# Weight splits as they land, output sums ahead of expert choice, token scales ahead of ranks, and the last routing in the count step's head

## The reference, cut to what matters

```python
x = L0_attn_x                                  # (4, 2048, 256)
xn = layernorm(x)
# gated linear attention, 8 heads, DK = 128, DV = 64
q = xn @ Wq ; k = (xn @ Wk) * DK**-0.5 ; v = xn @ Wv
alpha = sigmoid((xn @ Wg + bg) / 16)           # one per token and head
state = alpha_t * state + k_t (x) v_t          # over the 2048 tokens, in order
out_t = q_t . state
att = (out * sigmoid(xn @ Wog)) @ Wo
# mixture of experts: E = 64, 8 groups, the best 4 groups, the best 8 experts, CAP = 256
scores = sigmoid(xn @ gate_w.T) ; sfc = scores + gate_bias
# groups by the sum of their two best, then the best 8 experts among the 4 best groups
w = 2.5 * scores[chosen] / sum(scores[chosen])
# every expert takes its first 256 tokens of the 8192, in token order
ffn = sum over chosen experts of w * (silu(t @ w_gate) * (t @ w_up)) @ w_down
return x + att + ffn
```

## Time and profile before

| What | us |
|---|---|
| three runs, median (lowest to highest) | 1458.67 (1458.36 to 1460.96) |
| the profiled execution | 1454.37 |
| its span, first to last instruction | 1452.7 |
| mean granted TensorE clock, share of full | 0.976 |
| PE busy in the span | 1320.8 |
| DVE busy | 960.7 |
| ACT busy | 552.4 |

### The profile page before, as it was taken

One profiled execution on the slowest core, in us unless ns is written; L12 is line 12 of the kernel. 1 busy time (PEld: TensorE's weight loads), 2 busy tenths in 40 slices (PEclk: granted clock), 3 DMA queues, 4 the chain that ended last, 5 costly groups with the idle time before them and its releaser, 6 DMA issues.

```text
span 1452.7 us, 27616 instructions
## 1 busy us (share of the span) xinstructions
PE 1320.8 (91%) x9460; PEld 1143.8 (79%) x9460; DVE 960.7 (66%) x2425; ACT 552.4 (38%) x1079; POOL 530.6 (37%) x407
## 2 busy tenths in 40 slices
PE   2999888998989899989999999999999999999992
PEld 2778777786878687778888888888888888888872
DVE  4766777867775666857757577575775757757450
ACT  4555555545554342223333333333333333333220
POOL 3001001000100006735636456364563645636422
PEclk9989999999999999999999999999999999999996
DMA  5338433434332131125646566465564655646666
GB/s 201 128 124 266 137 122 125 163 106 135 124 136 96 66 94 59 59 84 152 150 138 154 130 152 148 135 154 133 148 147 136 156 135 154 151 140 151 178 216 219
DMA packets 134513, 203.48 MB, mean 140 GB/s; under 512 B 12400, under 2 KB 106160, under 8 KB 134320
## 3 DMA queue, kind: packets, MB, share of 16 engines
q1 hardware_dynamic: 108208, 161.10, 34.3%
q0 software_dynamic: 26240, 41.63, 14.9%
HBM read 153.33 MB, written 57.74 MB: 145 GB/s over the span
## 4 chain that ended last, share of the span: by engine, by line
PE 66%; DVE 15%; issue 6%; DMA 5%; ACT 4%; SPq 1%; POOL 1%; DVEq 1%; POOLq 0%; ACTq 0%
PE bank L672 16%; PE bank L791 6%; PE bank L747 6%; PE bank L767 6%; PE bank L684 5%; PE bank L714 4%; PE bank L732 4%; PE bank L800 4%; PE bank L696 3%; PE bank L735 3%; PE bank L705 3%; DMA out_dram<-arena 3%; DVE Dt L1251 2%; PE bank L617 2%; PE bank L781 2%
## 5 line engine op out<-in xcount | busy, mean ns | idle before, releaser
L540 POOL DMA_INDIRECT arena<-table,idx_all x132 | 167.7, 1270 | 271.6 <-DVE arena L1354 208.7
L548 POOL DMA_INDIRECT acc<-arena,idx_all x128 | 224.9, 1757 | 78.3 <-DMA acc<-arena,idx_all 42.2
L672 PE MATMUL bank<-xp,wq 128*128 128x512 f32 x768 | 210.2, 409 | 0.0
L672 PE MATMUL bank<-xp,wk 128*128 128x512 f32 x768 | 208.1, 407 | 0.0
L672 PEld LDWEIGHTS bank<-xp,wk 128*128 128x128 f32 x768 | 142.4, 192 | 32.0 <-issue 0.2
L1251 DVE TENSOR_TENSOR_SCAN Dt<-decay,eye_b 128x512 f32<-128x512 f32 x128 | 156.7, 1226 | 2.3 <-DMA decay<-decay_dram 2.3
L672 PEld LDWEIGHTS bank<-xp,wq 128*128 128x128 f32 x768 | 137.6, 191 | 25.5
L714 PE MATMUL bank<-qT,kT 128*128 128x128 f32 x1024 | 136.8, 277 | 2.7 <-ACT kT L954 2.7
L747 PEld LDWEIGHTS bank<-V,kw 128*128 128x128 f32 x960 | 121.0, 193 | 15.1 <-issue 10.6
L714 PEld LDWEIGHTS bank<-qT,kT 128*128 128x128 f32 x1024 | 125.2, 193 | 5.0 <-ACT kT L954 4.5
L747 PE MATMUL bank<-V,kw 128*128 128x64 f32 x960 | 128.2, 277 | 0.0
(11 more groups left out here) (152 smaller groups left out, 2200.0 us busy)
## 6 DMA issues: line engine op xcount, KB each, us to landing
decay<-decay_dram SPq DMA_DIRECT2D x64, 512.0 KB, 5.5
carry<-decay_dram SPq DMA_DIRECT2D x60, 512.0 KB, 4.6
arena<-in_L_attn_x_dram SPq DMA_DIRECT2D x16, 512.0 KB, 4.5
table<-arena SPq DMA_DIRECT2D x16, 512.0 KB, 3.0
xT_dram<-arena SPq DMA_DIRECT2D x16, 512.0 KB, 3.0
xs<-xT_dram SPq DMA_DIRECT2D x16, 512.0 KB, 5.3
arena<-in_L_ffn_w_gate_dram SPq DMA_DIRECT2D x64, 128.0 KB, 4.8
arena<-in_L_ffn_w_up_dram SPq DMA_DIRECT2D x64, 128.0 KB, 4.8
```

Source lines behind the costliest of these rows:

```text
L540: pool.indirect_dma_start(out=xg[:, e % 2, j, :], out_offset=None, in_=table[:, :], in_offset=bass.IndirectOffsetOnAxis(ap=idx_all[:, e, j ...
L548: pool.indirect_dma_start(out=acc[:, :], out_offset=bass.IndirectOffsetOnAxis(ap=idx_all[:, e, j:j + 1], axis=0), in_=yb[:, e % 2, j, :], ...
L672: last = mm(bank[which][:, :], w[:, part, k, h * DK:(h + 1) * DK], xp[:, other, k, :], start=(k + i == 0), stop=(k == KD - 1 and i == 2))
```

## The change

Four things are moved.

1. **The start.** Each weight has its own semaphore (`w_in_v` and so on). Raw og and o lie in `carry`, which is not written before step 1's first carries are loaded; SP waits for all five splits before it loads them. ACT takes the square root before it copies the router weights, and DVE no longer waits for the router constants before the first statistics. ACT makes v's high part while PE transposes, and the first tokens' high part straight from `xnT` (the trip through `xs` is gone for chunk 0). DVE makes all low parts, in the order v, tokens, q, k, og, o, with `gates(0)` and `decays_products(0)` between; POOL makes none. PE starts `proj_v(0, 0)` after v's split, does `decays_across(0)` after it, and waits for q, k and og one by one.
2. **Norm steps, DVE and ACT.** `scales(n)` now stands ahead of `route_ranks(n-1)` in all three places of a step. For s = 3 and 6, `std_of(n)` stands one place earlier on ACT, ahead of the copy of the next head's q.
3. **Norm steps, head, DVE.** `route_top(n-1)` stands behind `projected` 0 and 1 instead of ahead of them (a new place 4).
4. **The count step, DVE.** The four routing parts of chunk 15 stood in s = 1, behind the residual sums and the first scores; now `route_groups` and `route_ranks` stand at the head, ahead of `projected` 0 and 1, and `route_top` and `route_weights` right behind these two, ahead of the first scores.

Core of the diff:

```diff
-        raw["og"] = kT[:, :, :]
-        raw["o"] = og[:, 0:2, :].rearrange("p j n -> p (j n)").rearrange("p (k n) -> p k n", k=KO)
+        raw["og"] = carry_flat[:, 0:KD * HV].rearrange("p (k n) -> p k n", k=KD)
+        raw["o"] = carry_flat[:, KD * HV:KD * HV + KO * D].rearrange("p (k n) -> p k n", k=KO)
...
+                if first:
+                    sp.wait_ge(w_split, 5)
                 load_carry(c + 1, 0)
...
-            load_xs(0)
...
-            for name in ("og", "o"):
-                w = split_of[name][0]
-                pool.wait_ge(w_high, list(split_of).index(name) + 1)
-                pool.tensor_tensor(w[:, 1], raw[name], w[:, 0], ALU.subtract).then_inc(w_split_pool, 1)
...
                 pe.wait_ge(x_split, c + 1)
+                if first:
+                    pe.wait_ge(w_split, 1)
                 proj_v(c, 0)
+                if first:
+                    decays_across(0)
+                    pe.wait_ge(w_split, 2)
                 proj_qk(c, 0, 0)
                 beside(c, kind, 0, 1)
                 proj_v(c, 1)
+                if first:
+                    pe.wait_ge(w_split, 3)
                 proj_qk(c, 0, 1)
...
-                    if s % 3 == 0 and place == 1:
+                    if s % 3 == 0 and place == (0 if s > 0 else 1):
                         std_of(n)
...
+                        scales(n)
                         route_ranks(n - 1)
-                        scales(n)
+                    if s == 0 and place == 4:
                         route_top(n - 1)
                     if s in (3, 6) and place == 1:
+                        scales(n)
                         route_ranks(n - 1)
                         route_top(n - 1)
-                        scales(n)
...
                 if kind == "count" and s == 0 and place == 3:
-                    for part in (route_groups, route_ranks, route_top, route_weights):
-                        part(C - 1)
+                    route_groups(C - 1)
+                    route_ranks(C - 1)
+                if kind == "count" and s == 0 and place == 4:
+                    route_top(C - 1)
+                    route_weights(C - 1)
...
                     projected(c, 0, kind)
                     projected(c, 1, kind)
+                beside(c, kind, 0, 4)
```

51 lines of the change are left out of this document (30 added, 21 removed).

## The result

The changed kernel took **1410.6 us** (median; 1407.3 to 1413.6), the kernel before, run beside it, 1459.8: a ratio of 0.9661, 95% interval 0.9637 to 0.9685. The forecast was 1410.2 in a range of 1400 to 1424. The profiled execution took 1409.67, 1.7 of it around its span of 1408.0; before it was 1454.37 and 1452.7.

A forecast was written before the change was run, and what follows sets the result against it. PE bounds the kernel, busy 1320.8 of 1452.7 us, so only its waits and half-clock work can be won. Terms 5.8 + 8.7 + 16.3 + 3.0 + 6.4 + 8.3 = 48.5, off the 1458.67 median: 1410.2, range 1400 to 1424.

The forecast's parts named there:

- start: Path to step 0's decay scans: 7.7 us from an earlier decay DMA, less 1.9 lost, gives 5.8 us.
- step 0, middle: Step 0's stop for normalise goes and full clock returns, less a new stop's 0.2: 8.7 us.
- steps 1 to 4, with s = 7 and heads: Norm steps 1 to 4: middles 16.3, small waits 3.0 and residual-sum stops 6.4 us.
- s = 7: Late place in norm steps: three waits of 0.45 us and as many for the token copy go, 3.0 us.
- heads: Heads of steps 2 and 3: two residual-sum stops nearly go, plus step 2's low clock, 6.4 us.
- count step: Count step: the first count's 5.59 us stop goes, with 2.8 of half clock behind it, 8.3 us.
- everything up to the transposed tokens comes some 1.2 us earlier: At the start: statistics need not wait for router constants, so the second token copy ends at 13.7, not 14.88.
- k's low part: DVE subtract at the start: taken as 2.3 us, not 4.43; otherwise the start wins 4.5 in place of 7.7.
- (a): Rival: low clock stays after five 1.5 us stops and the start's; 1431 us, or 1415 from start alone; chance 0.09.
- (b): Rival: the stop in the middle of all five norm steps only moves to the token copy; 1435 us; chance 0.04.
- (c): Rival: the earlier square root makes ACT wait at ten places and starves PE of q; 1466 us; chance 0.02.
- (d): Rival: a hidden wait in the order keeps the old sequence, no gain; 1458.7 us; chance 0.01.

The follow-up runs named there:

- scales_only: Kernel before with only the norm-step move of token scales ahead of ranks, square root one place earlier: 1428.5 us, ratio 0.9813.
- pool_low: Changed kernel, but POOL makes og's and o's low parts again, ahead of its decay DMA: 1409.8 us, ratio 0.9667.
- warm36: Changed kernel with 36 extra matmuls, results unused, into a free bank ahead of step 0's fourth V part: 1409.0 us, ratio 0.9655.
- start_only: Kernel before with only the new start (part 1), the other three parts undone: 1451.3 us, ratio 0.9966.
- heads_only: Kernel before with only the expert choice moved behind the first two residual sums at norm-step heads (part 3): 1451.7 us, ratio 0.9965.
- gate_late: Changed kernel with the second output gate's sigmoid behind the token copies in the early steps: 1405.3 us, ratio 0.9638.
- std_late: Changed kernel with only the square root back in its old place, behind the q copy on ACT: 1409.4 us, ratio 0.965.
- v_first: Changed kernel, but in step 0 ACT copies the third and fourth V part ahead of the square root: 1405.7 us, ratio 0.9633.
- stats_first: Changed kernel, but DVE takes the second chunk's statistics ahead of the first scans, scales behind the first scan: 1404.5 us, ratio 0.9626.
- count_only: Kernel before with only the last routing moved to the head of the count step (part 4): 1451.9 us, ratio 0.9975.
- reordered: Changed kernel with step 0's square root, normalise, statistics and scales reordered, second gate's sigmoid late, query scaling ahead of ranks: 1396.4 us, ratio 0.9576.

## Why the prediction was right, step by step

**The sum.** By the step table, against the terms:

| term | predicted | measured |
|---|---|---|
| start | 5.8 | 5.7 alone; 4.6 at the first transposes |
| step 0, middle | 8.7 | 9.5, from the first transposes to step 1 |
| steps 1 to 4, with s = 7 and heads | 25.7 | 26.4 |
| count step | 8.3 | 8.3 |
| at the slots step | 48.5 | 48.8 |

The third line holds 19.6 (`scales_only`) for the 19.3 of middles and s = 7, and 6.7 for the 6.4 of the heads.

Every term was within 1.2 us, but the agreement of the sum to 0.3 us is partly luck: the start fell short by 1.2, and step 0 and steps 1 to 4 gave 0.8 and 0.7 more. The agreement of 1410.2 with 1410.6 holds luck too. The profiled execution was forecast at 1405.9 and took 1409.67, because its part from the slots step on was 4.1 us longer than before. The 4.3 us by which the median of before lay above its profiled execution are 0.9 in the changed kernel, and the two misses cancel.

**The start: the mechanism held, with a term mis-sized.** The changed kernel's ACT, DVE, POOL and PE at the start:

```profile
7.47 0.21 ACT L891 ACTIVATE arena<-arena 128x4 f32<-128x4 f32 x1 [5.25 <-DVE arena L1099]
8.80 0.28 ACT L939 ACTIVATE arena<-bank 128x128 f32<-128x128 f32 x1 [1.12 <-PE bank L595]
8.98 2.06 ACT L898 ACTIVATE arena<-arena 128x256 f32<-128x256 f32 x4
...
14.11 0.60 ACT L920 ACTIVATE arena<-bank 128x512 f32<-128x512 f32 x1 [1.20 <-PE bank L608]
```

```profile
17.69 2.29 DVE L1197 TENSOR_TENSOR wq<-Dt,wq 128x2048 fp32r<-128x2048 f32 x1 [0.65 <-ACT wq L935]
...
22.47 2.29 DVE L1197 TENSOR_TENSOR wk<-Dt,wk 128x2048 fp32r<-128x2048 f32 x1 [2.37 <-ACT wk L935]
...
25.45 0.06 DVE L1123 MEMSET arena<- 32x1 f32 x1
...
32.35 4.57 DVE L1263 TENSOR_TENSOR_SCAN Dt<-decay,eye_b 128x512 f32<-128x512 f32 x4 [2.01 <-DMA decay<-decay_dram]
```

```profile
26.16 0.58 POOL L511 DMA_DIRECT2D decay_dram<-arena  x1 [19.32 <-DVE arena L1123]
```

```profile
18.19 2.91 PE L680 MATMUL bank<-wv,xp 128*128 128x512 f32 x6
```

The step that failed is "everything up to the transposed tokens comes some 1.2 us earlier". The statistics did, at 5.35 instead of 6.36. But ACT's copy of the router weights stands ahead of `normalise`, and it needs PE's transposes of Wg, whose transfer landed only at 8.32. PE's first row:

```profile
8.32 0.44 PE L595 MATMUL bank<-ident,arena 64*128 64x64 f32 x2 [8.32 <-DMA arena<-in_L_attn_Wg_dram]
```

In the trace of before Wg had landed at 6.41. In the ten traces with the new start it lands between 7.76 and 9.10, in the four with the old one between 6.36 and 7.34; why it comes later is not shown. The second token copy starts at 14.11 against 14.28, so 0.2 of the 1.2 came. The decays are ready at 25.5 instead of 24.8. POOL's issue follows 0.65 behind, where I had let it follow at once, and from issue to scan it is 6.2 where I had 6.0. That puts the scan at 32.35 instead of 30.8 and the fourth V part at 39.68 instead of 38.1. From scan to V part it is 7.33, as before (38.51 to 45.84).

k's low part took 2.29 as taken, not 4.43, and `pool_low` shows why. The Trainium skill (GPSIMD Engine Reference, section Specifications) speaks of contention on shared interfaces where DVE has two SBUF inputs; the trace of `pool_low` agrees for such instructions, and there they ran one after the other.

The restart at half clock cost 1.6 (`warm36`), against 1.8. The start's gain at the first transposes is 4.6, 1.2 less than the term; that part 1 alone still moves step 1 by 5.7 goes with a shorter cold stretch behind the stop of step 0, which no term had: in `start_only` PEclk is 0.72, 0.50 and 0.70 over 72:77, 77:82 and 82:86 and then 1.00, where before it is 0.50 up to 88. This 0.9 is not the start's doing: `heads_only`, whose start is the old one, takes 64.1 us from the first transposes to step 1 as `start_only` does, and before takes 65.0.

**Step 0 and steps 1 to 4, middle.** PE at the second transposes of steps 1 and 4:

```profile
144.31 0.65 PE L608 MATMUL bank<-ident,arena 128*128 128x128 f32 x4 [1.65 <-ACT arena L920]
...
378.64 0.66 PE L608 MATMUL bank<-ident,arena 128*128 128x128 f32 x4 [1.47 <-ACT arena L920]
```

No wait for `normalise` (before), one of 1.44 to 1.66 for the token copy where 1.5 was said, and full clock at 75 to 88 us. The cause of that wait was only half seen: the ACT queue was one of two chains (`gate_late`).

**Rivals.** (a) did not come: none of the five short stops brought the low clock, and the start lost 1.6 and not 6.5. The Trainium skill (TensorE: Matmul & The Clock Gate, section Why this matters for your kernels) warns of idle stretches between bursts; the trace agrees for the 9.0 us stop. The stop of 2.26 us in `scales_only` brought the low clock too. Behind the five of 1.44 to 1.66 us, and behind one of 2.67 in the trace of before, the clock stayed full. (b) was excluded by `scales_only`, (c) by `std_late`, (d) by the four parts, each of which did what it says.

## What to carry to other kernels

- Price a stop as itself plus the half-clock work behind it, and look in the order for what is queued ahead of the one instruction that PE wants. Here that gave each term to within 1.2 us.
- In an in-order queue, an instruction that waits for another engine must not stand ahead of one whose data are there. The square root ahead of the V copy held PE for 9.0 us, of which `v_first` won back 1.9 and `stats_first` 5.9 by step 1; the router's copy ahead of `normalise` cost 0.9 at `normalise`.
- Before you move one of two chains that end close together, find the other: `gate_late` won in step 0 what it did not win in steps 1 to 4.

## What the runs showed of the hardware

- DVE and POOL instructions with two SBUF inputs ran in turns (`pool_low`, and the start of before). A DVE scan of 0.41 us took 2.28, and a TENSOR_TENSOR of 0.42 took 2.42, each ending 0.3 us behind POOL's.
- A stop's length alone does not tell whether the clock falls. Stops of 1.3 to 1.7 us in steps 1 to 4, between long stretches of work, never brought it. At the residual sum of step 3 it was one of 2.39 us (`count_only`) that did, and one of 2.67 (before) that did not. In step 0, the second V part took 1.67, 1.66 and 1.67 us behind stops of 1.52 (changed), 2.19 (`stats_first`) and 2.26 (`std_late`), and 2.50, 2.40, 2.45 and 2.81 behind stops of 1.80 (`v_first`), 1.75 (`reordered`), 1.77 (`pool_low`) and 1.97 (`warm36`). What decides there stays open.
- The low clock can last long after PE is back at work. Before, in step 0, it stood at half for 10 us in which PE was never idle:

```profile
78.00:88.00 10.00, 10.00 (x54) 9.34 (x54) 2.11 (x4) 2.40 (x8) 0.00 (x0) 0.50 0.62 210
```

  In the changed kernel, PE takes up work behind the 9.0 us stop at 39.68, and PEclk is 1.00 from 44 on. Why the one took so much longer stays open, so the price of a stop's low clock can't be carried from one place to another.
